# Keys and values of 41 batches formed from high and low parts, split by GpSimd

## The reference, cut to what matters

```
def _L1_xattn_ref(Q, K, V, Wq, bq, Wk, bk, Wv, bv, Wo, bo):     # K = V = ctx_1024 (64, 257, 256)
    q = _split_heads(Q @ Wq.T + bq)
    k = _split_heads(K @ Wk.T + bk)
    v = _split_heads(V @ Wv.T + bv)
    scores = jnp.einsum('bhqd,bhkd->bhqk', q, k) * scale
    ...
x = x + _L0_xattn_ref(...)      # stage a0
x = x + _L0_attn_ref(...)       # delta rule: stages b0s (solve), b0g (gates), b0m (mix)
x = x + _L0_ffn_ref(...)        # 8 experts, 2 for a token: router f0r, experts f0
x = x + _L1_xattn_ref(...)      # uses the keys and values formed ahead
...
```

## Time and profile before

| | before |
|---|---|
| median of three runs | 1634.19 us |
| the profiled execution: time | 1632.93 us |
| its span | 1631.10 us |
| mean granted clock of TensorE | 0.97 of full speed |
| PE busy | 1495.9 us |
| DVE busy | 1099.4 us |
| ACT busy | 812.2 us |
| POOL busy | 585.6 us |

### The profile page before, as it was taken

How to read it: one execution, slowest core, us unless ns; L and a number is a source line. 1 busy time by engine, 2 the same in 40 slices (tenths; PEclk the granted TensorE clock), 3 DMA queues, 4 the chain that set the end, 5 groups by cost and what they waited for, 6 DMA issues and landing times. The chain is left out here.

```text
span 1631.1 us, 38596 instructions
## 1 busy us (share of the span) xinstructions
PE 1495.9 (92%) x15236; PEld 1160.9 (71%) x15236; DVE 1099.4 (67%) x2415; ACT 812.2 (50%) x1847; POOL 585.6 (36%) x487
## 2 busy tenths in 40 slices
PE   6897989899998999999999888999799688999998
PEld 4444467555576579999998746666688677799997
DVE  4687879982047555565562567888599677668787
ACT  1233742121134336666663448999277322666664
POOL 2430300000011027676654256787288452121210
PEclk9999989999999999999999999999999798999999
DMA  9991059621024367666648416664000010000001
GB/s 324 357 349 49 1 172 216 129 56 46 1 78 136 95 219 251 224 254 247 250 173 202 115 44 229 209 204 142 27 1 1 17 30 16 0 27 27 27 1 52
DMA packets 114075, 203.97 MB, mean 125 GB/s; under 512 B 38073, under 2 KB 74361, under 8 KB 108009
## 3 DMA queue, kind: packets, MB, share of 16 engines
q1 hardware_dynamic: 91481, 107.69, 22.3%
q0 software_dynamic: 10032, 57.55, 10.1%
q10 hardware_dynamic: 12384, 36.27, 6.8%
HBM read 161.63 MB, written 39.83 MB: 124 GB/s over the span
## 5 line engine op out<-in xcount | busy, mean ns | idle before, releaser
L2369 POOL TENSOR_TENSOR a_pr<-a_pr,a_inv 128x1028 f32<-128x1028 f32 x64 | 122.2, 1910 | 63.8 <-DVE a_inv L2496 63.8
L380 PE MATMUL ps<-kv_ctx,kv_w 128*128 128x257 f32 x464 | 125.1, 406 | 7.2 <-PEq L1577 2.4
L384 PE MATMUL ps<-kv_w,kv_ctx 128*128 128x256 f32 x464 | 118.0, 399 | 11.6 <-ACT kv_kv L404 11.6
L2460 ACT ACTIVATE a_pr<-ps,a_neg 128x257 f32<-128x257 f32 x256 | 119.0, 473 | 1.7 <-DVE a_neg L2512 1.7
L1613 POOL TENSOR_TENSOR b0m_pm<-b_dr,b_gates 128x256 f32<-128x256 f32 x16 | 13.2, 831 | 290.3 <-SPq L1577 261.4
L2512 DVE TENSOR_REDUCE a_neg<-ps 128x2 f32<-128x514 f32 x128 | 87.8, 688 | 39.9 <-PE ps L2386 38.9
L384 PEld LDWEIGHTS ps<-kv_w,kv_ctx 128*128 128x128 f32 x464 | 89.9, 200 | 32.9 <-ACT kv_kv L404 18.8
L380 PEld LDWEIGHTS ps<-kv_ctx,kv_w 128*128 128x128 f32 x464 | 88.0, 201 | 25.9 <-issue 10.5
L3366 DVE SCALAR_TENSOR_TENSOR x<-ps,g_gate,x 128x256 f32<-128x256 f32 x256 | 105.1, 475 | 0.0
L2397 PE MATMUL ps<-ident,a_pr 128*128 128x128 f32 x512 | 81.2, 282 | 17.0 <-ACT a_prT L2467 11.6
L964 DVE SCALAR_TENSOR_TENSOR b_F<-b_F,b_fir 128x992 f32<-128x992 f32 (+29 forms) x128 | 96.5, 790 | 0.0
(11 more groups left out here) (442 smaller groups left out, 4444.2 us busy)
## 6 DMA issues: line engine op xcount, KB each, us to landing
late_kv<-kv SPq DMA_DIRECT2D x52, 513.0 KB, 4.2
kv<-kv_kv ACTq DMA_DIRECT2D x46, 513.0 KB
a_ctxT<-in_ctxT SPq DMA_DIRECT2D x32, 514.0 KB, 8.9
a_ctxR<-in_ctx SPq DMA_DIRECT2D x32, 512.0 KB
kv_ctx<-in_ctxT ACTq DMA_DIRECT2D x34, 257.0 KB
kv_ctx<-in_ctxT SPq DMA_DIRECT2D x24, 257.0 KB
outs<-f_yo SPq DMA_DIRECT2D x16, 256.0 KB
a_vB<-vlast SPq DMA_DIRECT2D x32, 128.0 KB
```

The costliest lines, as they stand in the source:

```text
L380: done = e.matmul(out[:, 0:NK], self.w[:, 0, c, cols(part)], ctx[:, c, :], start=(c == 0), stop=(c == DC - 1))
L384: done = e.matmul(out[:, cols(t, D)], ctx[:, c, cols(t)], self.w[:, 1, c, :], start=(c == 0), stop=(c == DC - 1))
L2369: e.tensor_tensor(pr[:, b % RP, :, :], pr[:, b % RP, :, :], inv[:, b % 2, :].unsqueeze(2).to_broadcast([P, HG, NK]), ALU.mult).then_inc(*p ...
L2460: e.activation(pr[:, b % RP, r, :], K.ps[:, bank(b, r), 0:NK], ACT.Exp, bias=neg[:, b % 2, r:r + 1], accum_out=tot[:, b % 2, r:r + 1]).the ...
```

## The change

Of the 64 batches, those with numbers 4 to 44 (41 of them) are formed by `product3`: 24 matmuls on fp32r operands instead of 8 on fp32 ones, with 258 columns instead of 257 for the keys, since the context is padded to an even number of columns (`NKE`). Batches 0 to 3 and 45 to 63 stay as they were. GpSimd splits the operands: `split_weights` once (a cast and a subtraction of 128 x 1024), and `split` for each batch (a cast and a subtraction of 128 x 516). The high part goes into one of two buffers, so the split of batch b waits until batch b-2 has been formed on PE; the low part is written over the fp32 operand, in the same slot or, for the weights, in the same place (`Room(Y, "kvraw")` gives both one address). PE's first job of a batch waits for the batch's low part instead of the context's load. Since the later batches need the fp32 weights again, SP loads them a second time in the experts' stage, behind a wait for batch 44. The array `ab` now shares the place of `beta`, and the descriptors' scratch of the DMAs that GpSimd issues is set to 8192 bytes.

```diff
+    def split_weights(self, e):
+        e.wait_ge(*self.ld_w.at(48))
+        e.wait_ge(*self.mm.at(3 * self.FIRST_SPLIT))
+        high, low = self.w_parts
+        e.tensor_copy(high[:, :, :, :], self.w[:, :, :, :]).then_inc(*self.w_split.up())
+        e.wait_ge(*self.w_split.at(1))
+        e.tensor_tensor(low[:, :, :, :], self.w[:, :, :, :], high[:, :, :, :].bitcast(F32), ALU.subtract).then_inc(*self.w_split.up())
+
+    def split(self, e, n):
+        for b in range(self.parted, self.parted + n):
+            s, high = self.slot_of[b], self.ctx_high[b % 2]
+            e.wait_ge(*self.ld_c[s].at(16 * (len(self.before(b)) + 1)))
+            if b - self.FIRST_SPLIT >= 2:
+                e.wait_ge(*self.mm.at(3 * (b - 2) + 3))
+            e.tensor_copy(high, self.ctx[s]).then_inc(*self.high.up())
+            e.wait_ge(*self.high.at(b - self.FIRST_SPLIT + 1))
+            e.tensor_tensor(self.ctx_low[s], self.ctx[s], high.bitcast(F32), ALU.subtract).then_inc(*self.low.up())
+        self.parted += n
...
-            if part == 0:
+            if part == 0 and in_parts:
+                e.wait_ge(*self.low.at(b - self.FIRST_SPLIT + 1))
+            elif part == 0:
                 e.wait_ge(*self.ld_c[s].at(16 * (len(self.before(b)) + 1)))
...
+            if in_parts and part < 2:
                 for c in range(DC):
-                    done = e.matmul(out[:, 0:NK], self.w[:, 0, c, cols(part)], ctx[:, c, :], start=(c == 0), stop=(c == DC - 1))
+                    done = product3(e, out[:, 0:NKE], [t[:, 0, c, cols(part)] for t in w], [t[:, c, :] for t in x], c == 0, c == DC - 1)
+            elif in_parts:
+                for t in range(2):
+                    for c in range(DC):
+                        done = product3(e, out[:, cols(t, D)], [q[:, c, cols(t)] for q in x], [q[:, 1, c, :] for q in w],
+                                        c == 0, c == DC - 1)
...
+            @block.gpsimd                       # b0s
+            def _(e):
+                ahead.split_weights(e)
+                ahead.split(e, 21)
...
             @block.gpsimd                       # b0m
             def _(e):
+                ahead.split(e, 2)
                 for t in range(NT):
                     if t >= 2:
                         e.wait_ge(*v_a0.at(t - 1))
                     e.tensor_tensor(by_head(pm[:, t % 2, 3, :]), by_head(dr[:, t, :]), gate(t, 2), ALU.mult).then_inc(*p_p3.up())
+                    if t % 2 == 0 and ahead.parted < AHEAD[2] + ahead.FIRST_SPLIT:
+                        ahead.split(e, 1)
...
+                A.split(e, 9)                   # f0, GpSimd, ahead of its gathers
                 e.wait_ge(*v_row.at(3))
                 gather1(0)
                 gather1(1)
                 e.wait_ge(*st_r.at(16 * NT))
                 gather2(0)
+                A.split(e, 1)
                 e.wait_ge(*v_token.at(1))
                 gather_rows(0)
                 gather_rows(1)
+                A.split(e, 1)
...
                 A.sync(e, AHEAD[3] - 3)         # f0, SP
+                A.load_weights_again(e)
...
-    nc = bacc.Bacc("TRN2", target_bir_lowering=False, num_devices=1)
+    nc = bacc.Bacc("TRN2", target_bir_lowering=False, num_devices=1, dynamic_dma_scratch_size=8192)
```

More of the change, by code:

```diff
@@ L43 @@
 FIRSTS, HALVES = zip(*block_chunks())
+NKE = NK + NK % 2
 KV = 2 * NK + 2 * D
@@ L318 @@
     BY_SYNC, TAIL, QUERIES = sum(AHEAD[:3]) + SLOTS, sum(AHEAD[:4]), sum(AHEAD[:5])
+    FIRST_SPLIT = sum(AHEAD[:2])
     def __init__(self, Y):
         self.K, self.Y = Y.K, Y
-        self.w, self.bk = Y.sb("w", [P, 2, DC, D]), Y.sb("bk", [P, DC])
-        self.ctx = places(Y.sb("ctx", [P, self.SLOTS, DC, NK]))
+        with Room(Y, "kvraw") as Z:
+            self.w, ctx = Z.sb("w", [P, 2, DC, D]), Z.sb("ctx", [P, self.SLOTS, DC, NKE])
+        w_low, ctx_low = Y.sb("wL", [P, 2, DC, D], F32R), Y.sb("ctxL", [P, self.SLOTS, DC, NKE], F32R)
+        self.w_parts = [Y.sb("wH", [P, 2, DC, D], F32R), w_low]
+        self.ctx, self.ctx_low = places(ctx), places(ctx_low)
+        self.ctx_high = places(Y.sb("ctxH", [P, 2, DC, NKE], F32R))
+        self.bk = Y.sb("bk", [P, DC])
         self.ld_w = Y.sig("dma", "wkv")
@@ L329, in __init__ @@
         self.mm, self.ev = Y.sig("pe", "kv"), Y.sig("act", "kv")
+        self.w_split, self.high, self.low = Y.sigs_of("pool", "kvw kvhigh kvlow")
         self.own = [KvPlace(Y, at, f"kv{n}") for n, at in enumerate(places(Y.sb("kv", [P, 2, KV])))]
         self.formed = self.taken = self.last = 0
+        self.parted = self.FIRST_SPLIT
         self.hosts = []
@@ L347, in load @@
         s = self.slot_of[b]
-        e.dma_start(self.ctx[s], self.K.ins["ctxT"][b // BT, :, b % BT, :, :]).then_inc(*self.ld_c[s].up(16))
+        e.dma_start(self.ctx[s], self.K.ins["ctxE"][b]).then_inc(*self.ld_c[s].up(16))
     def sync(self, e, n):
@@ L377, in pe @@
                 e.wait_ge(*self.ev.at(j - many + 1))
-            if part < 2:
+            if in_parts:
+                w, x = self.w_parts, [self.ctx_high[b % 2], self.ctx_low[s]]
+            if in_parts and part < 2:
                 for c in range(DC):
-                    done = e.matmul(out[:, 0:NK], self.w[:, 0, c, cols(part)], ctx[:, c, :], start=(c == 0), stop=(c == DC - 1))
+                    done = product3(e, out[:, 0:NKE], [t[:, 0, c, cols(part)] for t in w], [t[:, c, :] for t in x], c == 0, c == DC - 1)
[4 more added lines that the diff above has]
+                                        c == 0, c == DC - 1)
+            elif part < 2:
+                for c in range(DC):
+                    done = e.matmul(out[:, 0:NK], self.w[:, 0, c, cols(part)], ctx[:, c, 0:NK], start=(c == 0), stop=(c == DC - 1))
             else:
@@ L1003, in delta_attention @@
         rn = sb("rn", [P, NT, 8])
-        cb, ab = (sb(n, [P, NT, H0]) for n in ("cb", "ab"))
+        cb, ab = sb("cb", [P, NT, H0]), beta
         ld_b, ld_f, ld_2 = Y.sigs_of("dma", "beta fir rest")
```

15 lines of the change are left out of this document (13 added, 2 removed).

## The result

The changed kernel takes 1698.47 us, the median of five runs (1687.41 to 1698.93), against 1634.19 (1625.51 to 1638.25). The ratio is 1.0383, 95% interval 1.0347 to 1.042: slower, by 64 us. The forecast was 1684, range 1652 to 1706.

A forecast was written before the change was run, and what follows sets the result against it. It took DVE to set the Gram loop, PE the later solve, and hand-overs among all engines the mixing loop; 1632.93 + 21.7 (b0s) + 26 (b0m) + 4 (Router) - 1 (The rest) = 1683.6, forecast 1684 us, range 1652 to 1706.

The forecast's parts named there:

- b0s: Delta rule's solve up to DVE's first outputs: POOL's splits block DVE's filter taps, +21.7 us (ends 0 and +30).
- d - 0.15: Cost to a DVE operation reading two SBUF tensors of a POOL operation lasting d: 1.6 us a batch, weights 3.5.
- The slack: DVE's waits for PE in the solve that could absorb blocking: 3.6 us in the Gram loop, 3.93 behind it.
- b0m: Mixing loop: splits in POOL's queue cost +22 us over seven rings and +4 ahead of the first product, +26 together.
- the ring: Mixing loop's closed chain of waits through POOL, DVE, ACT and PE, once every two tiles: 9.0 us, against 5.82 before.
- The two leading splits: Two splits on POOL ahead of the mixing loop's first product: 2 x 1.9 = +4 us.
- Router: Router and the stage behind: first job's wait +2, blocked DVE +5, PE's savings -3: +4 us (ends -2 and +10).
- The rest: Remaining jobs of the solve and another stage: -1 us; second weights load, smaller scratch and `ab` over `beta`: 0.
- (1): Rival: POOL doesn't block DVE, only the ring in the mixing loop costs: 1660 us, chance 18%.
- (3): Rival: PE sets the Gram loop, POOL's work costs nobody, mixing loop hides splits: 24 us less, 1609, chance 4%.
- (4): Rival: gathers stall in the smaller scratch, 13 us more than the forecast: 1697 us, chance 3%.
- (2): Rival: POOL suffers beside DVE too, a batch taking 2.6 us on POOL and 2.3 on DVE: 1703 us, chance 9%.

The follow-up runs named there:

- e10: Kernel before plus, for each of the 41 batches, two POOL memsets nobody reads, in the splits' places; products from fp32, weights still split: 1678.66 us, one execution.
- e6: Changed kernel plus 26 unused 256-column matmuls on PE behind the transposes of each even mixing-loop tile from 2 on: 1705.64 us, ratio 1.0394.
- e2: Kernel before with the 41 batches formed by the cheaper products from high parts cast once, all other splits left out: 1624.78 us, ratio 0.9941.
- e5: Changed kernel without any split, all batches formed from fp32, the change's other parts kept: ratio 0.9991 to the kernel before.
- e1: Changed kernel with POOL splitting a fixed operand for nobody, all batches formed from fp32, second weights load left out: 1692.78 us, ratio 1.036.
- e8: As e1, but POOL's subtraction for each batch replaced by a second cast, which reads one tensor: 1685.70 us, one execution.
- e9: Changed kernel with no splits ahead of the mixing loop's first products, later ones behind odd products, 18 filler matmuls ahead of the router's count: 1689.75 us, ratio 1.0318.
- e3: Changed kernel with each mixing-loop split behind the odd product instead of the even one: 1667.76 us, ratio 1.0201.

## Why the prediction was right

The mechanism was right in both places, and the sum came out 14 us low against the median, 4 against the profiled execution, in part by luck.

- **b0s**, +21.7 forecast, +20.6 measured. The price by d - 0.15 was a little high, above all for the weights (3.5 us, by e10 0.8): 35.5 us of splitting less what lies beside PSUM reads, 29.2, were to lengthen DVE's work, and 24.8 did. The slack it could eat was smaller too, 4 us for 7.5, since in the Gram loop PE waited for splits. The two errors cancel.
- **b0m**, +26 forecast, +33.4 in the loop and +1.8 ahead of it. The term that was mis-sized is the ring: 9.0 us said, 10.5 measured. The sum of its steps left out the key job ahead of the values (12 matmuls stood there, there are 18, 0.72 us), and took 0.12 us a matmul, which holds at full clock only: e6 puts 1.0 us on the clock. Seven rings make 10 us too little. The two leading splits cost 4.3 us (the first begins at 493.1, the product at 497.4), as said; 2.5 of it came back in the gates' stage ahead, from which only a part of 1 was expected.
- **Router**, +4 forecast, +8.3 measured. What POOL's work costs DVE was about right (5 said, 4.4). The -3 for PE's savings holds for the cheaper products by themselves (-2.8 in e2), but not beside splits: there the experts chosen come later and the cheaper jobs no longer cover the wait, PE stood for 2.24 us and fell to the lower clock for the count that DVE waited for. The sum added two effects that act on each other.
- **The rest**, -1 forecast, -13 in this trace. e5, which splits nothing, measures about 0 for the change's other parts, and the traces differ by more than 13 us among themselves there (1016 to 1048 us). So nothing shows it to be of the change, and here luck comes in: with a rest as long as before the profiled execution would lie 16 us above the forecast and not 4. The +3.4 us ahead of the first Gram product, where nothing was forecast, are of the same kind (-1 to +5 in the other traces).
- **Rivals.** (1), no blocking, falls by e1; (3) by e1 and e2; (4) by e5. Of (2), POOL suffering as well, a part is true: its subtraction took 1.70 us on average in the solve, not 1.28, and its cast 0.81.
- The Trainium skill's rule ("SBUF — State Buffer", section "Who interferes with whom") agrees with e1 and e8 in who is held up: taps with two inputs in SBUF are, products out of PSUM are not. That whoever issues first keeps the pair for its whole instruction the section writes of DVE's two-port modes; of a two-input operation it says only that it contends. The whole-instruction price of 1.9 us a batch would have given 6 us more, 28 against the 20.6 measured. It names GpSimd's reads, and not its writes, for a two-input operation, and e10 agrees: memsets, which read nothing, cost 0.

## What to carry to other kernels

An idle engine isn't free help: see what its operations read and which operations of its neighbour run beside them, and price the pair by one overlapped pair of rows. In a queue that somebody waits on, put work that itself waits behind the product that is waited for, never ahead of it; here one product's place was worth 24 us. And don't add up the effects of two changes that meet at one wait: the cheaper jobs cost nothing alone, nor did TensorE's clock fall for the count with the splits alone, but together they left TensorE idle ahead of it, and it came out of the wait at half its clock.

## What was not expected

- GpSimd's operation must read: 40 memsets beside the same taps cost DVE 0 us, 40 casts some 12 (13 with the weights). The theory of e10 had it otherwise.
- DVE's tensor_scalar, with one tensor in SBUF, suffers too: the 128x32 one above took 1.28 us for 0.17 beside POOL's work. The prediction priced operations with two inputs alone; the same section of the Trainium skill counts tensor_scalar among those that may take the shared pair, in their two-port modes; whether this one ran in such a mode no trace shows.
- In e5's and e9's traces PE stands in the last experts' stretch, and from the first matmul on gathered rows to the next layer they take 17 and 29 us longer than the trace of before. The rows are waits of e5 between 860 and 960 us:

```profile
PEld ps L432 <- issue: 17.3, 8, 4.7
ACT kv_kv L458 <- remote: 11.8, 2, 6.6
```

  PE's jobs need a bank that ACT has emptied, and ACT, before it takes values out of PSUM, waits for something that the trace calls "remote" and doesn't name; in e9 four such waits make 28 us. The next layer's first step stands behind it in ACT's queue: DVE waits 23.7 us for it in e5 and 29.4 in e9, where that wait is 1.0 in the trace of before and 0.4 in the changed kernel's. What holds ACT up stays open. It isn't the splits, which e5 doesn't make. The smaller scratch, the layout and the second load are in e5 too, so its trace alone doesn't clear them; the traces of the changed kernel and of e3, which have them as well, show no such stall. Whether it is what spreads the executions of every kernel here, the one before too (1620 to 1652 us over the three groups), no trace shows.
